# Edge batches of fourteen tiles as a triangle, counts by accumulator, low one-hots on ScalarE

## What is computed

```python
def _gcn_conv(h, row, col, ew, dis, W, b):
    xw = h @ W
    norm = dis[row] * ew * dis[col]
    agg = segment_sum(norm[:, None] * xw[row], col, N)
    return agg + (dis * dis)[:, None] * xw + b
ew  = clip(abs(_safe(edge_weight)), 1e-06, None)
deg = segment_sum(ew, col, N) + 1.0;  dis = rsqrt(deg)
...
x = x + L0_gnn(layernorm(x), edge_index, edge_weight)   # two GCN layers
x = x + L0_ffn(layernorm(x))                            # top 2 of 8 experts
x = x + L1_gnn(layernorm(x), edge_index, edge_weight)   # five gated layers: segment_sum(m[src] * edge_attr, dst), GRU
x = x + L1_ffn(layernorm(x))
```

## Time and profile before

| | us |
|---|---|
| median of 3 runs | 3950.57 (3947.44 to 3955.93) |
| the profiled execution | 3948.2 |
| its span in the trace | 3946.3 |
| PE busy | 3061.4 (78%) |
| DVE busy | 2372.5 (60%) |
| POOL busy | 1453.3 (37%) |
| ACT busy | 1294.5 (33%) |

### The profile page before, as it was taken

How to read it: one execution, slowest core, us unless ns; L and a number is a source line. 1 busy time by engine, 2 the same in 40 slices (tenths; PEclk the granted TensorE clock), 3 DMA queues, 4 the chain that set the end, 5 groups by cost and what they waited for, 6 DMA issues and landing times. The chain is left out here.

```text
span 3946.3 us, 55029 instructions
## 1 busy us (share of the span) xinstructions
PE 3061.4 (78%) x18296; PEld 2758.0 (70%) x18297; DVE 2372.5 (60%) x5595; ACT 1294.5 (33%) x2337; POOL 1453.3 (37%) x922
## 2 busy tenths in 40 slices
PE   2555553200699995999958999999999999999798
PEld 2444442100588884888848998998998899899678
DVE  7999994411488777555565545555545545555447
ACT  0000000110344452333324444444444444444255
POOL 1567888877767677677730000000000000000000
PEclk9999997655799997999989999999999999999879
DMA  9876333577566766445344433343333443334100
GB/s 397 266 215 190 44 43 46 133 192 195 135 173 169 207 167 154 129 103 143 56 135 170 139 118 125 128 130 125 129 117 117 136 129 117 125 129 135 41 30 28
DMA packets 381098, 538.45 MB, mean 136 GB/s; under 512 B 126115, under 2 KB 283978, under 8 KB 377482
## 3 DMA queue, kind: packets, MB, share of 16 engines
q1 hardware_dynamic: 251076, 487.82, 36.6%
q0 software_dynamic: 119088, 19.33, 8.7%
q10 hardware_dynamic: 10774, 29.17, 2.1%
HBM read 398.99 MB, written 137.24 MB: 136 GB/s over the span
## 5 line engine op out<-in xcount | busy, mean ns | idle before, releaser
L495 POOL DMA_INDIRECT plane_a<-pair,slot x392 | 650.6, 1660 | 285.4 <-issue 121.9
L501 POOL DMA_INDIRECT plane_w<-pair,slot x392 | 669.4, 1708 | 231.0 <-issue 119.9
L601 PE MATMUL bank<-ring_hi,h_hi 128*128 128x448 f32 x1750 | 652.0, 373 | 59.8 <-DVE ring_lo L1677 54.3
L1677 DVE TENSOR_TENSOR ring_lo<-ring_lo,ring_hi 128x448 fp32r<-128x448 f32 x875 | 522.1, 621 | 218.7 <-ACT ring_hi L1088 218.4
L601 PE MATMUL bank<-ring_lo,h_hi 128*128 128x448 f32 x1750 | 642.2, 367 | 0.0
L601 PE MATMUL bank<-ring_hi,h_lo 128*128 128x448 f32 x1750 | 641.9, 367 | 0.0
L1088 ACT ACTIVATE ring_hi<-ring_lo 128x448 fp32r<-128x448 f32 x875 | 497.1, 576 | 381.0 <-PE bank L601 374.7
L549 POOL DMA_DIRECT2D v_lo<-gru_v x5 | 3.6, 724 | 1383.5 <-PE bank L601 1308.6
L601 PE MATMUL bank<-gring_hi,hs_hi 128*128 128x512 f32 (+2 forms) x700 | 261.8, 374 | 276.6 <-DVE gring_lo L1392 276.6
L601 PEld LDWEIGHTS bank<-ring_hi,h_hi 128*128 128x128 f32 x1750 | 330.8, 189 | 87.7 <-DVE h_lo L1744 48.2
L574 PE MATMUL bank<-parts,eq 128*128 (+1 forms) x3136 | 132.4, 170 | 319.3 <-DVE hit_hi L1340 319.1
(11 more groups left out here) (342 smaller groups left out, 6191.7 us busy)
## 6 DMA issues: line engine op xcount, KB each, us to landing
ring_lo<-plane_w SPq DMA_DIRECT2D x175, 1120.0 KB, 5.4
gring_lo<-plane_a SPq DMA_DIRECT2D x50, 1280.0 KB, 6.0
plane_a<-nat SPq DMA_DIRECT2D x25, 1600.0 KB, 44.9
plane_w<-nat SPq DMA_DIRECT2D x100, 400.0 KB
w_hl<-w_split SPq DMA_DIRECT2D x16, 2048.0 KB
keyrow<-key_rows ACTq DMA_DIRECT2D x49, 512.0 KB, 3.9
part_in<-in_L_ffn_W SPq DMA_DIRECT2D x16, 1024.0 KB, 10.2
w_split<-part_hi SPq DMA_DIRECT2D x16, 1024.0 KB, 4.4
```

Of the source, the lines that this page charges most:

```text
L495: g_.indirect_dma_start(out=plane, out_offset=bass.IndirectOffsetOnAxis(slot[:, t:t + 1], 0), in_=pair[:, k, t:t + 1], in_offset=None, com ...
L501: g_.indirect_dma_start(out=plane_w, out_offset=bass.IndirectOffsetOnAxis(slot[:, n:n + 1], 0), in_=pair[:, 0, n:n + 1], in_offset=None, c ...
L601: last = mm(ps, lhs[x], rhs[y], start=start and n == 0, stop=stop and n == 2)
L1677: V.tensor_tensor(ring_lo[:, t, :], ring_lo[:, t, :].bitcast(FP32), ring_hi[:, t % HS, :].bitcast(FP32), ALU.subtract).then_inc(lo_rdy, 1)
```

## The change

A batch has 14 tiles, so there are 28. `eq` keeps only a triangle: tile q of a batch is compared with the tiles 0 to q. The comparison with the earlier tiles is one instruction per q whose accumulator gives the count of earlier equals in earlier tiles (`before_n`); the diagonal block is a second one. PE multiplies 105 blocks of 6 or 8 columns. The count inside the own tile comes from a column of powers of two in `parts0` and a threshold (`order`, `beyond`), so `own`, `before` and `parts1` go. The low one-hots are made by ACT as Relu(1 - (row - dlo)^2), two dependent activations a tile, in `mark_low`. keyrow has two buffers. The constants that pace fills, parts and plane_w scatters are set anew: 19 plane_w scatters lie among the batches, 252 come before the expert stage and 140 in it.

```diff
-G = 8
-KB = 4
+G = 14
+KB = 2
 NB = ET // G
-W1 = 32
-FB, FIRST_W = 8, 17
-BP, P0 = 30, 4
+UP = G * (G + 1) // 2
+W1 = 18
+FB, FIRST_W = 13, 9
+BP, P0 = 18, 4
...
-                sp.wait_ge(scat_a, 16 * G * (BP + n))
+                sp.wait_ge(scat_a, 16 * G * (BP + n // 2))
...
             def sum_batch(n, c):
                 pe.wait_ge(compared, n + 1 + KB)
+                pe.wait_ge(lo_hit, n + 1)
                 pe.wait_ge(sums_out, n + 1)
                 for g in range(G):
-                    for q in range(G):
-                        parts = (parts1 if q < g else parts0)[:, bass.ds(n * G + q, 1), :].rearrange("p a k -> p (a k)")
-                        mm(ps_sum[c][:, g, :], eq[:, c, q, g * EP:(g + 1) * EP], parts, start=(q == 0), stop=(q == G - 1))
+                    parts = lambda q, cols: parts0[:, bass.ds(n * G + q, 1), 0:cols].rearrange("p a k -> p (a k)")
+                    mm(ps_sum[c][:, g, :], eq_row(c, g, g, g + 1), parts(g, 8), start=True, stop=(g == G - 1))
+                    for q in range(g + 1, G):
+                        mm(ps_sum[c][:, g, 0:6], eq_row(c, q, g, g + 1), parts(q, 6), start=False, stop=(q == G - 1))
...
+            def mark_low(n, c):
+                act.wait_ge(summed, n + 1)
+                for g in range(G):
+                    act.wait_ge(lo_apart, n * G + g + 1)
+                    A(off_lo[:, g % 2, :], row[:, :], ACT.Square, bias=dlo_neg[:, bass.ds(n * G + g, 1)]).then_inc(lo_apart, 1)
+                    act.wait_ge(lo_apart, n * G + g + 2)
+                    last = A(hit_lo[:, c, g, :], off_lo[:, g % 2, :], ACT.Relu, bias=1.0, scale=-1.0)
+                last.then_inc(lo_hit, 1)
...
             with act.Fori(0, LOOPED) as i:
                 for b in range(KB):
                     load_keys(KB * (i + 1) + b, b)
+                    mark_low(KB * i + b + 1, (b + 1) % 2)
                     take_sums(KB * i + b, b % 2)
...
                 at = lambda x, g: x[:, bass.ds(n * G + g, 1)]
+                for q in range(G):
+                    if q > 0:
+                        V.tensor_scalar(eq_row(c, q, 0, q), keyrow[b][:, 0:q * EP], at(key, q), None, ALU.is_equal, ALU.add, accum_out=before_n[:, c, q:q + 1])
+                    V.tensor_scalar(eq_row(c, q, q, q + 1), keyrow[b][:, q * EP:(q + 1) * EP], at(key, q), None, ALU.is_equal)
                 for g in range(G):
-                    V.tensor_scalar(eq[:, c, g, :], keyrow[:, b, :], at(key, g), None, ALU.is_equal)
-                for g in range(G):
-                    V.scalar_tensor_tensor(own[:, c, g, :], keyrow[:, b, g * EP:(g + 1) * EP], at(key, g), before[:, :], ALU.is_equal, ALU.mult, accum_out=own_n[:, c, g:g + 1])
-                for g in range(G):
-                    V.tensor_scalar(hit_lo[:, c, g, :], row[:, :], at(dlo, g), None, ALU.is_equal)
                     last = V.tensor_scalar(hit_hi[:, c, g, :], row[:, 0:NT], at(dhi, g), at(wabs, g), ALU.is_equal, ALU.mult)
                 last.then_inc(compared, 1)
...
-                link(V.tensor_tensor(earlier[:, c, :], sums[:, c, :, 6], own_n[:, c, :], ALU.add))
+                link(V.scalar_tensor_tensor(earlier[:, c, :], sums[:, c, :, 6], beyond[:, 0:1], before_n[:, c, :], ALU.is_gt, ALU.add))
```

More of the change, by code:

```diff
@@ L163, in build @@
         lo_i, hi_i, spare_i = (early[:, m, :].bitcast(I32) for m in (5, 6, 7))
-        srci = sb("srci", [EP, ET], I32); dsti = sb("dsti", [EP, ET], I32); w = sb("w", [EP, ET])
+        w = sb("w", [EP, ET])
         wabs = sb("wabs", [EP, ET]); key = sb("key", [EP, ET])
[L166 to L169, removed]
+        dhi = dstf
+        to_spare = sb("to_spare", [EP, ET])
+        parts0 = sb("parts0", [EP, ET, 8], BF16)
+        order_i = sb("order_i", [EP, 1], I32); order = sb("order", [EP, 1]); beyond = sb("beyond", [EP, 1])
         hit_lo = sb("hit_lo", [EP, 2, G, 128]); hit_hi = sb("hit_hi", [EP, 2, G, NT])
-        own = sb("own", [EP, 2, G, EP], BF16); own_n = sb("own_n", [EP, 2, G])
+        dlo_neg = sb("dlo_neg", [EP, ET]); off_lo = sb("off_lo", [EP, 2, 128])
+        before_n = sb("before_n", [EP, 2, G])
         sums = sb("sums", [EP, 2, G, 8]); half = sb("half", [EP, 2, G, 2])
@@ L174, in build @@
         scope.append(ExitStack())
-        keyrow = sb("keyrow", [EP, KB, G * EP])
-        eq = sb("eq", [EP, 2, G, G * EP], BF16)
+        eq = sb("eq", [EP, 2, UP * EP], BF16)
+        eq_row = lambda c, q, lo, hi: eq[:, c, (q * (q + 1) // 2 + lo) * EP:(q * (q + 1) // 2 + hi) * EP]
         scope.pop().close()
@@ L181, in build @@
         spare = xT[:, :, :].rearrange("p k n -> p (k n)")
+        keyrow = (front[:, 0:G * EP], spare[:, KD * NP - G * EP:KD * NP])
+        keyT = eq[0:ET // 4, 0, 0:8 * EP].bitcast(FP32).rearrange("t (c p) -> t c p", c=4)
+        srci, dsti = (eq[:, 1, 2 * ET * n:2 * ET * (n + 1)].bitcast(I32) for n in range(2))
         wt_sb = spare[:, 0:LAYERS * KD * D].rearrange("p (i k f) -> p i k f", i=LAYERS, k=KD)
@@ L471, in _ @@
             g_ = nc.gpsimd
-            g_.memset(srci[:, :], NP - 1).then_inc(padded, 1)
-            g_.memset(dsti[:, :], NP).then_inc(padded, 1)
+            g_.memset(srci, NP - 1).then_inc(padded, 1)
+            g_.memset(dsti, NP).then_inc(padded, 1)
             g_.memset(w[:, :], 0.0).then_inc(padded, 1)
@@ L478, in _ @@
             g_.memset(ident[:, :], 0.0).then_inc(consts, 1)
-            g_.memset(before[:, :], 1.0).then_inc(consts, 1)
+            g_.iota(order_i[:, :], [[0, 1]], base=187, channel_multiplier=-1).then_inc(consts, 1)
             g_.memset(below[:, :], 1.0).then_inc(consts, 1)
@@ L561, in _ @@
             mm(ps_deg, zeros[:, 0:128], zeros[:, 0:NT], start=True, stop=False)
-            pe.wait_ge(consts, 10)
+            pe.wait_ge(consts, 9)
             pe.wait_ge(key_done, 1)
@@ L923, in take_sums @@
                 A(sums[:, c, :, :], bank[c][0:EP, 0:8 * G].rearrange("p (g k) -> p g k", k=8), ACT.Copy).then_inc(sums_out, 1)
+            act.wait_ge(lo_ready, 1)
+            act.sem_inc(lo_apart, 1)
+            mark_low(0, 0)
             LOOPED = (NB - KB) // KB
@@ L928, in _ @@
                     load_keys(KB * (i + 1) + b, b)
+                    mark_low(KB * i + b + 1, (b + 1) % 2)
                     take_sums(KB * i + b, b % 2)
             for n in range(KB * LOOPED, NB):
-                if n + KB < NB:
-                    load_keys(n + KB, (n + KB) % KB)
+                if n + 1 < NB:
+                    mark_low(n + 1, (n + 1) % 2)
                 take_sums(n, n % 2)
@@ L1353, in _ @@
             compare(0, 0, 0)
-            with ch.loop(0, NB // KB, 2 * KB) as i:
+            LOOPED = NB // KB - 1
+            with ch.loop(0, LOOPED, 2 * KB) as i:
                 for b in range(KB):
@@ L1357, in _ @@
                     place(KB * i + b, b % 2)
-            place(NB - 1, (NB - 1) % 2)
+            for n in range(KB * LOOPED, NB):
+                if n + 1 < NB:
+                    compare(n + 1, (n + 1) % KB, (n + 1) // KB)
+                place(n, n % 2)
             def rest_of_part(n):
```

27 lines of the change are left out of this document (14 added, 13 removed).

## The result

The kernel after takes 3879.6 us (median of 4 runs, 3878.4 to 3884.3) against 3949.2 for the kernel before (4 runs, 3947.4 to 3955.9): ratio 0.982, 95% interval 0.9806 to 0.9834. The forecast was 3890 in a range of 3868 to 3925. The profiled execution took 3878.4 us, its span is 3876.7, so 69.6 us of span (3946.3 before) are to be accounted for.

What follows compares the result with a forecast made beforehand. POOL's scatters were taken to end the edge stage and to pace the expert stage. From 3948.2 us, 59 for the earlier GCN panel and 3 for the expert stage gave 3886, plus 4 for safety 3890; range 3868 to 3925.

Steps and rivals of the forecast that it cites:

- The rival with the fast form: DVE's accumulating comparison keeps 0.53 ns a column, DVE ends at 505 us, tile 252 releases the parts: 3891 us, chance 0.15.
- DVE's batch: DVE's work per batch of fourteen in the edge stage: 21.0 us, against 15.9 with the cheaper accumulator.
- The slow form: DVE's accumulating comparison costs 1.04 ns a column, 0.139 + 0.133 q us for q blocks; chance 0.5.
- the rival with a costlier batch: DVE's long accumulating rows carry a drain or port wait, 0.08 us a row, 29 us in all: 3919 us, chance 0.22.
- Start and tail of DVE: DVE's edge work starts at 50 us, waits 9.5 us before the last place and ends at 648 us.
- Parts' chain: SP's weight parts, from part 0's store at 657 us, take 299.7 us and release the GCN panel at 957.
- POOL's end: POOL's last plane_a scatter lands at 943 us, ahead of the panel; tile 252 has landed at 644.
- the 0.03 us a scatter for short operations: Extra time of POOL's edge-stage scatters that DVE's short operations still cause when the accumulating comparison is slow.
- contention: DVE's wide comparisons slow POOL's 253 scatters up to 670 us by 0.11 us each, 28 us; probably mostly gone.
- The slower rival: ACT's 28 handshakes of mark_low bound the edge loop, deciding from 0.72 us an activation: up to 3990 us, chance 0.05.
- The expert stage: POOL paces it: four more plane_w scatters cost 7.5 us, fewer landing waits save 11.7; counted as -3 us.
- The safety of 4 us: Added to the sum of 3886 us because the loads' start and DVE's step are more likely longer than shorter.

Runs made afterwards that it cites:

- the kernel with the parts ahead: The kernel after with each weight part loaded one step earlier, ahead of the store of the part before it: 3872.5 us, 0.980 of the kernel before.
- the first experiment: The kernel after with the low one-hots made by DVE again instead of ACT: 3957.2 us, 1.002 of the kernel before.
- with 19: The kernel after with W1, the plane_w batches scattered before the experts, raised from 18 to 19: 3864.5 us, 0.978 of the kernel before.
- with 20: The kernel after with W1, the plane_w batches scattered before the experts, raised from 18 to 20: 3866.0 us, 0.978 of the kernel before.

## Why the prediction was right, point by point

The time alone would not have shown it. The rival with the fast form gave 3891, the forecast 3890, so what tells them apart are the rows: comparisons of 1.94 us, scatters of 1.55 beside them, the parts' start at 643 and not 505, the panel behind the parts and not behind POOL. And two misses of nearly 6 us, the panel earlier than forecast and the way from there to the gathers longer, cancel by luck.

- **What bounds the stage.** POOL before, the parts after: both as put. The panel was forecast at 957 and went out at 951.1.
- **DVE's batch.** 21.0 us forecast, 20.9 measured. The slow form was the choice that carried it: own's two-source row of 128 columns gave the price of a one-source row of 1664 (0.139 + 0.133 x 13 = 1.87; the step from 61.61 to 63.48 is 1.87, and the read lies beside the next row, so the drain that the rival with a costlier batch feared isn't there). The Trainium skill (SBUF — State Buffer, "Who interferes with whom") keeps the accumulating form of tensor_scalar out of the two-port mode. The trace agrees: 1.04 ns a column against 0.53 for the plain form, and scatters of 1.55 us beside it against 1.67. One figure behind the forecast was read loosely: 2.29 us for 2048 columns is 1.12 ns a column by division and 1.02 as a slope from own's 0.34 us for 128, where 1.04 was written.
- **Start and tail of DVE.** 47.1 against 50; the last wait 10.6 against 9.5. End 643.1 against 648.
- **Parts' chain.** 299.7 us forecast from part 0's store to the panel, 298.5 measured. So most of the 6 us by which the panel came earlier than forecast are the 5 at DVE's end.
- **POOL's end.** 943 forecast for the last landing, some 933 measured (930.5 and the 3.0 us that the panel stood behind the last scatter in the kernel with the parts ahead); the 299 us behind tile 252 were right (298), the time up to it was not (644 against 635). The step that failed is the 0.03 us a scatter for short operations: the scatters up to there are 1.55 us each, which is 8 us, and the start was 2.9 earlier; odd gaps of 9 us instead of 6.5 took some of it back. It cost nothing, as the parts bind. Of contention 28 us were forecast, 8 of them to stay; 31.0 went in the experiment that kept the batch of eight, and 28.2 in the kernel after.
- **ACT.** 8.9 us a batch, inside the bounds of 7.8 to 14.8 and hidden under 20.9. The slower rival wanted 0.72 us an activation; it is 0.32. What it takes off DVE is worth 78 us in this kernel, by the first experiment. PE's sums wait for DVE's hit_hi and never for the low one-hots.
- **From the panel to the first gather.** Forecast unchanged, measured +5.6. ACT's first rounding of a panel starts 9.3 us after the load's issue (960.31 against 951.06), where before it was 5.9. The panel now leaves right behind the last weight stores and ten small loads instead of 38 us after them, and that explains these 3.4 us: in the four kernels where the last small load goes out 0.5 us ahead of the panel the rounding starts 8.9 to 9.7 us behind the panel's issue, in the six where it goes out 38 us or more ahead, 5.8 to 5.9 (5.89 with the parts ahead). The other 2 stay open.
- **The expert stage.** This is the term that was mis-sized: -3 forecast, -8.5 measured. The landing waits were scaled by the number of batch boundaries (26.8 to 15); they fell to 8.6. Before, 12 of the 17 boundaries in the stage waited, 2.2 us each; after, 5 of 10, 1.7 us each. What counts is where a boundary falls, and that can be followed through the loop at line 537. In the kernel before, 9 of the 17 stand right behind another plane_w scatter, and all nine waited (1.7 to 5.9 us, 20.0 in all); of the 8 right behind a gather or a result scatter three did (6.7 in all). In the kernel after, 5 of the 10 stand right behind a plane_w scatter, and these five waited (1.6 to 1.9) and the others did not. A gather or result scatter in between gives the landing time to finish. So W1 changes the waits by shifting the boundaries too (12.4 us with 19, 8.7 with 20). POOL's own sum then closes the term: 5.9 us for four more scatters, 3.3 more issue gaps, 18.2 less landing waits, -9. Two boundaries of the kernel after, the first behind a result scatter and the second behind a plane_w scatter:

```profile
1574.89 0.99 POOL L528 DMA_INDIRECT chosen<-xT,idx_y  x1 [0.30 <-issue]
1576.19 1.60 POOL L504 DMA_INDIRECT plane_w<-pair,slot  x1 [0.30 <-issue]
...
1613.75 1.61 POOL L504 DMA_INDIRECT plane_w<-pair,slot  x1 [0.30 <-issue]
1616.99 1.56 POOL L504 DMA_INDIRECT plane_w<-pair,slot  x1 [1.63 <-DMA plane_w<-pair,slot]
```

- **The safety of 4 us** went the wrong way. The sum without it was 3886; 3879.6 is 6 below that.

## What to carry to other kernels

Ask which chain ends last after the change, not only before it: here the same edit on ACT was worth nothing in one kernel and 78 us in the other, because the larger batch had moved DVE's end from 503 us (the new operations with batches of eight) to 643 and onto the path. Where an engine issues one long series of scatters through several stages, its idle time ahead of a stage is a budget; move work into it until it is just used up, for beyond that every scatter is paid at the start of the stage. Leave room: the first 14 scatters cost 45 us of idle time here, where 29 were expected, and the next 14 cost 25. And a serialised landing wait costs per boundary, so larger batches pay even where the per-item work stays the same (39.5 us from eight to fourteen), and less where other work of the same queue stands right ahead of the boundary (the expert stage).

## What the runs showed of the hardware

- An accumulating tensor_scalar takes 1.04 ns a column (0.34 us for 128, 1.94 for 1664 f32 columns) where the plain one takes 0.53, with a read of the accumulator of 0.08 us. Beside it an indirect DMA issued by POOL keeps POOL busy for 1.55 us on average, beside the plain form at 1024 columns for 1.67 and up to 1.85. Plain comparisons of 128 columns, which stand between the accumulating ones, add nothing to the 1.55.
- The wait for a scatter to land, in front of the next batch, is not a constant: 2.1 us on average with batches of fourteen (27.0/13), 2.5 before, 2.9 with the new operations and batches of eight. Over the first boundaries alone, where no plane_w scatter stands in between, it is 2.55 (20.4/8), 2.5 (38.0/15) and 3.1 (50.3/16). That shorter scatters leave more of the landing to be waited for would explain the last figure; it wasn't tested.
- Another indirect DMA of POOL between the last scatter and the wait covers that wait in most cases: in the expert stage of the kernels before and after all 14 boundaries behind a plane_w scatter waited, and of the 13 behind a gather or a result scatter three.
- Speeding up one stream of transfers slowed another: the parts one step ahead added 9.6 us to POOL's scatters and their waits, and put the last scatter 6.6 to 9.7 us later in three pairs of kernels.
- The same 1176 to 1344 matmuls on PE took 241.0 or 245.7 us (272.7 or 278.0 for the longest piece) in executions of nearly the same kernel, with the granted clock at 1.00 in the third piece at either pace.
